# A graph kernel whose zero blocks are written in 512-byte pieces

## What is computed

```
# layer 0: attention over the edges
k, q, v = typed_linear(x, Wk/Wq/Wv, node_type)          # 8 heads of 16
a  = (rel_att[etype](k[src]) * q[dst]).sum(-1) * rel_pri / 4
m  = rel_msg[etype](v[src])
h  = segment_sum(m * softmax_over_dst(a), dst)          # then Wa, gate, LayerNorm, residual, LayerNorm
# layer 1: three graph convolutions with batch norm
norm = dinv[src] * ew * dinv[dst]
h = segment_sum((h @ W)[src] * norm, dst) + b           # x 3; ReLU after the first two
out = layernorm(x + h)
```

## Time and profile before

| | |
|---|---|
| median of two executions | 4587.36 us |
| the profiled execution | 4592.19 us |
| its span, first to last instruction | 4590.3 us |
| busy share of the span: PE, DVE, ACT, POOL | 65%, 50%, 25%, 53% |
| granted TensorE clock, mean | 0.823 |
| zeros written (`a_tab<-stage`, SP) | 49 DMAs of 1,792 KB, issued 408.1 to 1205.9 us |
| gathers from `kv_tab` (POOL) | 832 DMAs, issued 409.0 to 2094.4 us |
| scatters to `a_tab` (POOL) | 416 DMAs, issued 1284.2 to 2517.1 us |

### The profile page before, as it was taken

The page is one execution under the profiler, slowest core; times in us unless marked ns, Lnnn a source line. Parts: engine busy times, 40 slices in busy tenths (PEclk is TensorE's granted clock), DMA queues, the critical chain, the costliest instruction groups (busy, mean ns, idle before and its releaser), DMA issues. The chain is left out here.

```text
span 4590.3 us, 52237 instructions
## 1 busy us (share of the span) xinstructions
PE 2969.0 (65%) x14449; PEld 2143.5 (47%) x14449; DVE 2312.5 (50%) x8186; ACT 1147.0 (25%) x2512; POOL 2411.3 (53%) x2514
## 2 busy tenths in 40 slices
PE   3895666666676666664420666777767776767774
PEld 3774656666666656663200433344433444433342
DVE  3774655655655555553522345533455534455435
ACT  1223556555655555552001200000000000000001
POOL 0002544444466666665577266665466664666662
PEclk9998778777787877776755889988899988999987
DMA  4896555565422322221000455555545545555552
GB/s 110 273 358 232 199 200 210 189 216 191 163 88 80 87 79 81 84 81 48 1 1 0 172 190 174 189 191 184 186 174 190 189 174 179 192 188 176 189 189 61
DMA packets 232026, 706.47 MB, mean 154 GB/s; under 512 B 62326, under 2 KB 111957, under 8 KB 212928
## 3 DMA queue, kind: packets, MB, share of 16 engines
q1 hardware_dynamic: 104252, 447.79, 26.7%
q0 software_dynamic: 93184, 191.21, 14.4%
q10 hardware_dynamic: 34308, 64.13, 4.3%
HBM read 559.66 MB, written 143.28 MB: 153 GB/s over the span
## 5 line engine op out<-in xcount | busy, mean ns | idle before, releaser
L552 POOL DMA_INDIRECT stage<-h_tab,earr x1248 | 1183.3, 948 | 810.8 <-issue 346.5
L527 POOL DMA_INDIRECT arena<-kv_tab,idxr x832 | 796.0, 957 | 970.3 <-ACT idxr L634 405.6
L1013 PE MATMUL bank<-arena,xr 128*128 128x512 f32 (+1 forms) x2058 | 1021.1, 638 | 5.6 <-issue 5.6
L992 PE MATMUL bank<-oh,stage 128*128 128x128 f32 x2496 | 394.3, 308 | 494.0 <-issue 487.8
L992 PEld LDWEIGHTS bank<-oh,stage 128*128 128x128 f32 x2496 | 354.1, 214 | 712.3 <-issue 701.1
L860 PE MATMUL bank<-xr,arena 128*128 x3328 | 494.0, 308 | 236.8 <-DVE arena L1254 146.9
L1572 DVE TENSOR_TENSOR sums<-sums,bank 128x128 f32 x1248 | 351.3, 282 | 568.3 <-remote 398.2
L1013 PEld LDWEIGHTS bank<-arena,xr 128*128 128x128 f32 x2058 | 407.6, 212 | 394.8 <-issue 394.8
L860 PEld LDWEIGHTS bank<-xr,arena 128*128 128x128 f32 x3328 | 456.0, 218 | 259.3 <-issue 258.2
L499 POOL DMA_INDIRECT a_tab<-tot,cell x416 | 416.0, 1000 | 261.2 <-DMA arena<-kv_tab,idxr 151.1
L709 ACT ACTIVATE rs<-mv,epsc 128x49 f32<-128x49 f32 (+1 forms) x6 | 1.9, 316 | 2003.3 <-DVE mv L1611 1692.6
(11 more groups left out here) (224 smaller groups left out, 2739.4 us busy)
## 6 DMA issues: line engine op xcount, KB each, us to landing
arena<-a_tab SPq DMA_DIRECT2D x147, 1792.0 KB
a_tab<-stage SPq DMA_DIRECT2D x49, 1792.0 KB
kv_tab<-stage SPq DMA_DIRECT2D x48, 768.0 KB, 8.5
arena<-key_d ACTq DMA_DIRECT2D x52, 512.0 KB, 7.1
arena<-ew_d ACTq DMA_DIRECT2D x52, 512.0 KB, 10.1
arena<-rel_d SPq DMA_DIRECT2D x52, 512.0 KB
stage<-h_tab,earr POOLq DMA_INDIRECT x1248
arena<-kv_tab,idxr POOLq DMA_INDIRECT x832
```

The source lines that it names most:

```text
L527: G.indirect_dma_start(kv[b % 3][:, t, :], None, kv_tab, bass.IndirectOffsetOnAxis(idxr[:, b % 3, t:t + 1], 0))\
L552: G.indirect_dma_start(gring[:, (q % NG) * GRP + s, :], None, h_tab[l], bass.IndirectOffsetOnAxis(src_i[:, t:t + 1], 0)).then_inc(row_land ...
L992: last = M.matmul(bank[q % NG][:, s * P:(s + 1) * P], gring[:, (q % NG) * GRP + s, :], oh[:, q % NG, s, :], start=True, stop=True)
L1013: mm = M.matmul(o_[:, 0:cw], xr[:, n, :], abuf[B % NBUF][:, n % KB, 0:cw], start=n == 0, stop=n == NT - 1)
```

## The change

The zero transfer's source becomes the first 128 words of the strip, read 28 times over, and the destination is written as 28 pieces of 128 words per partition in place of 4 pieces of 896. The number, the bytes, the order and the semaphores of the transfers are as before.

```diff
                     for z in range(zeros_by(b - 1), zeros_by(b)):
-                        sp.dma_start(a_flat[z, :, :].rearrange("p (a f) -> p a f", a=4),
-                                     zero.rearrange("p (a f) -> p a f", a=1).to_broadcast([P, 4, ZW]))\
+                        sp.dma_start(a_flat[z, :, :].rearrange("p (a f) -> p a f", f=P),
+                                     zero[:, 0:P].rearrange("p (a f) -> p a f", a=1).to_broadcast([P, KB * 512 // P, P]))\
                           .then_inc(a_zeroed[z // BPC], 16)
```

## The result

The kernel after takes 4625.81 us (two executions, 4622.03 and 4629.59) against 4587.36 before: ratio 1.0081, 95% interval 1.0055 to 1.0107. It is 38 us slower, 0.8%, where 65 us faster was forecast. The profiled execution has a span of 4627.7 us, 37.4 more than before.

The account below looks back on a forecast made before the run. POOL's chain of gather, landing, gather was taken as the bound. The period would fall from 31.88 to 27.28 + 2 x 1.0 = 29.3 us, saving 2.6 x 25 = 65 us: median 4522 us, 80% range 4478 to 4635.

Parts of the forecast that it names:

- What bounds the loop: Attention loop: POOL's chain of gather, landing, gather sets the period; zeros cost 4.6 us a burst, 115 us in all.
- Length of a burst: Zero burst of two transfers: 13.5 us instead of 9.6, at 30 ns a 512-byte piece, hidden.
- Delay of the gathers: POOL's gathers beside a zero burst: some 30 pieces stand ahead, so the delay falls from 4.5 to 0.9 us.
- The second group: POOL's next gather group in the batch: the longer burst reaches it too and delays it by 0.9 + 0.1 us.
- SP's own queue: Second zero transfer and rel load on SP: 5 to 10 us to issue, covered, so 0 us cost.
- the joined pieces: Rival, chance 0.25: zero pieces are joined, gather delay stays 3.3 to 4.5 us, burst 12.4 us; 4587 to 4625 us.
- What is held in bytes or by transfer: Rival, chance 0.10: 107 KB or one transfer stands ahead of a gather, first landing wait 1.8 us longer; 4657 us.

Follow-up runs that it names:

- experiment 1: All 49 zero transfers issued ahead of the attention loop instead of two per batch, against the kernel before: ratio 1.0192, 4421 us for 4338.
- experiment 2: Zero pieces of 512 (the kernel after), 1,792, 7,168 and 14,336 bytes against 3,584 in the kernel before: ratios 1.0067, 0.9981, 1.0030, 1.0116.

## Why the prediction was wrong, point by point

- *What bounds the loop.* Right. POOL's landing waits set the period, in the kernel after and in every experiment with bursts in the loop. One reading of it is off: 16 x 1.25 + 3 x 2.7 = 28.1 counts the 0.30 us of issue also where a wait takes its place. It is 16 x 0.95 + 13 x 0.30 + 8.1 = 27.2, so no wait is hidden; the quiet period and the price of the zeros, 4.6 us a burst, were confirmed by the zeros issued ahead (experiment 1).
- *Length of a burst.* Right: 28.5 ns a piece for the 30 of the save of h, 101.5% of the engines' time. The Trainium skill, "DMA: Bandwidth & Descriptors", section "Why small descriptors are slow (HBM only)", charges some 3 cycles a packet, and the estimate by it was 1.16 times the time; the two windows show 383 and 1.01 MB / 3.5 us = 289 GB/s, 1.33 times. The measurement decides.
- *Delay of the gathers.* **This step failed.** The prediction said "what is ahead of a gather is counted in pieces, 30 x 30 ns = 0.9 us replaces 4.5". One size of piece gave one number, 4.5 us, and I divided it by the piece to get a depth. Five sizes make it some 3.5 us that don't depend on the piece plus about 5.6 pieces (experiment 2). The delay fell only to 3.6 for the first group, a term of 0.8 us a batch in place of 3.6. The load of x had a hint of the constant in it, a gather behind small rows that had moved nothing 5.3 us after its issue, and I used it for another rival.
- *The second group.* Named rightly: the longer burst reaches it. It was priced at 1.0 us because the delay was; it took 2.7 (5.3 less 2.6). Sum by the measured terms, with waits of 6.2 and 5.3: 31.88 - 0.8 + 2.7 = 33.8, where 33.42 was measured (1.54 more than before).
- *SP's own queue.* Right: 5.9 and 6.3 us to issue, and hidden.
- *The rivals.* The upper end of the joined pieces, 4625, is the measured time, but by luck: the packet count shows single pieces, and the burst reached the second group by 2.7 us, not by 0 to 1.5. Its guess of a delay nearly as now (3.3 to 4.5) was the better one. What is held in bytes or by transfer is refuted too: the first wait would have grown, it fell. The Trainium skill, same page, section "Queues, rings and completion order", has an engine change queues after 9 to 17 descriptors; the estimate by it was 0.3 to 0.5 us. The trace shows 3.5 us, the time of some 120 small pieces, so that rule does not describe the wait.

Still open is what the 3.5 us are. By the fit they don't depend on the piece, they were smaller with 28 short DMAs, and they lie before the gather's last packet, not in its landing. Why the packets go late (their descriptors come late, or the engines prefer the queue that they are on) no run here tells apart. Zeros over another queue were not tried.

## What to carry to other kernels

A delay that is known at one size only is a sum with unknown terms; dividing it by the size makes a depth out of a constant. Before cutting transfers into small pieces so that others get between them, look for a second size in the trace, and count what the longer burst will reach. Where a burst hurts a chain of waits, its place and its order in the queue were worth more than its form: 51 us by a wait and a swap of two DMAs together (14 by the wait alone, none by the swap alone), against a loss of 38 by the pieces. And an engine that starts to wait is not yet the bound: look whether the engine that sets the period waits for it.

## What was not expected of the hardware

- Write pieces of 512 bytes ran at 28.5 ns per piece and engine (289 GB/s over 16), 3,584-byte ones at 150 ns (383 GB/s).
- Two transfers of 3,584 pieces hold SP's queue for 5.9 us, and a DMA behind them for 6.3.
- A gather beside a backlog of another queue is late by about 3.5 us and the time of 5.6 pieces, from 512 to 14,336 bytes (bursts of two transfers of 1,792 KB). With 128 KB DMAs issued one by one, at 97% busy engines, it lost 1.4 to 2.2.
- The late gather's packets go late (none in the 4.3 us of 751:755.3 in the kernel after); from its last packet to POOL's next gather it is 1.2 us, for 1.1 without a burst.
